# A two-block convolution on one core: a buffer of its own for each batch of d, its high part made by GpSimd, and a load of x without slots to wait for

## What is computed

```python
def _L0_conv_ref(x, p1, p3, p4, p5, p6):
    t1 = jnp.einsum('nchw,he->ncew', x, p1)             # h 32 -> e 16
    t2 = stack of x shifted by -1, 0, 1 rows            # 3c rows
    t3 = depthwise conv 9x9 of t1 with p3
    t4 = grouped conv 5x1 of t3 with p4, c // 4 groups
    t5 = jnp.einsum('ncew,ewf->ncf', t4, p5[:, :, 0, :])
    t6 = depthwise conv 1x3 of t5 along f with p6
    out = jnp.einsum('ncf,nfp->ncp', t6, t2) / sqrt(3c)

def _L1_conv_ref(x, conv_w, gamma, beta):
    cH, cV, cD = haar details of x; each upsampled bilinearly
    y = jnp.einsum('bchw,oc->bohw', concat([x, up(cH), up(cV), up(cD)]), conv_w)
    out = relu(batch norm of y * gamma + beta)

x = x + _L0_conv_ref(_gn(x), ...)
x = x + _L1_conv_ref(_gn(x), ...)
```

## Time and profile before

| | us |
|---|---|
| Median of 3 runs | 372.99 |
| Lowest, highest | 367.62, 376.11 |
| The profiled execution, its own time | 367.42 |
| Its span (first to last instruction) | 365.5 |
| TensorE, VectorE busy | 289.2, 294.2 |
| ScalarE, GpSimd busy | 215.3, 182.7 |

### The profile page before, as it was taken

One profiled execution on the slowest core, in us unless ns is written; L12 is line 12 of the kernel. 1 busy time (PEld: TensorE's weight loads), 2 busy tenths in 40 slices (PEclk: granted clock), 3 DMA queues, 4 the chain that ended last, 5 costly groups with the idle time before them and its releaser, 6 DMA issues.

```text
span 365.5 us, 4713 instructions
## 1 busy us (share of the span) xinstructions
PE 289.2 (79%) x1560; PEld 233.3 (64%) x1560; DVE 294.2 (81%) x539; ACT 215.3 (59%) x317; POOL 182.7 (50%) x186
## 2 busy tenths in 40 slices
PE   4566759999894994999989999999999999873000
PEld 0000129999783994567778888888888888651000
DVE  4899977985891862357668999999999999979792
ACT  3444665665963854364565667776676666530891
POOL 7454670050440040302487888888888888842000
PEclk9999998999999896999999999999999999995555
DMA  7979814589359761589000000000000000000399
GB/s 187 245 186 237 239 44 131 175 264 273 109 136 312 256 166 35 134 320 385 3 2 0 2 0 2 2 0 0 2 1 2 0 2 2 0 0 1 154 402 363
DMA packets 18344, 43.59 MB, mean 119 GB/s; under 512 B 2992, under 2 KB 7344, under 8 KB 18320
## 3 DMA queue, kind: packets, MB, share of 16 engines
q1 hardware_dynamic: 16928, 41.00, 36.6%
q0 software_dynamic: 960, 2.09, 2.3%
q10 hardware_dynamic: 432, 0.21, 0.2%
HBM read 30.44 MB, written 8.39 MB: 106 GB/s over the span
## 4 chain that ended last, share of the span: by engine, by line
DVE 48%; PE 21%; issue 8%; DMA 7%; SPq 6%; ACT 6%; POOL 3%; DVEq 0%; POOLq 0%; ACTq 0%
PE wide L637 10%; DVE xa L770 5%; DVE st L878 5%; DMA d_sb<-t_out 5%; DVE x_sb L983 4%; DVE x_sb L871 4%; DVE y_sb L917 4%; SPq L276 4%; DVE sty L923 3%; DVE sty L759 3%; DVE d_split L784 2%; DVE y_sb L910 2%; DVE u_sb L854 2%; DVE u_sb L846 2%; DVE u_sb L863 2%
## 5 line engine op out<-in xcount | busy, mean ns | idle before, releaser
L637 PE MATMUL wide<-t_all,s_hi 128*128 128x272 f32 x320 | 50.2, 306 | 15.5 <-ACT s_hi L465 12.9
L637 PEld LDWEIGHTS wide<-t_all,s_hi 128*128 128x128 f32 x320 | 45.2, 202 | 18.4 <-ACT s_hi L465 14.6
L778 DVE TENSOR_TENSOR s_lo<-s_f,s_hi 128x768 fp32r<-128x768 f32 x32 | 32.1, 1002 | 24.9 <-ACT s_hi L465 24.8
L429 POOL TENSOR_TENSOR g_lo<-y_sb,g_hi 128x1024 fp32r<-128x1024 f32 x15 | 36.2, 2411 | 14.4 <-ACT y_sb L562 14.4
L561 ACT ACTIVATE g_hi<-x_sb,rs 128x1024 fp32r<-128x1024 f32 x16 | 21.4, 1340 | 33.8 <-POOL rs L414 33.8
L607 PE MATMUL bank<-xa,p_blk 128*64 128x512 f32 x64 | 28.2, 979 | 14.8 <-DVE xa L770 14.8
L233 PE MATMUL wide<-g_hi,t_hi 128*128 128x512 f32 x96 | 38.0, 395 | 0.7 <-DVE t_lo L898 0.7
L276 POOL DMA_DIRECT2D d_sb<-t_out x24 | 13.3, 560 | 50.3 <-ACT t_out L479 43.9
L235 PE MATMUL wide<-g_hi,t_lo 128*128 128x512 f32 x96 | 37.7, 393 | 0.0
L234 PE MATMUL wide<-g_lo,t_hi 128*128 128x512 f32 x96 | 37.7, 392 | 0.0
L770 DVE STREAM_TRANSPOSE xa<-x_slot 128x1024 f32<-128x1024 f32 x16 | 31.6, 1993 | 6.6 <-DMA x_slot<-in_x 6.3
(11 more groups left out here) (130 smaller groups left out, 815.8 us busy)
## 6 DMA issues: line engine op xcount, KB each, us to landing
s_f<-in_taps SPq DMA_DIRECT2D x32, 384.0 KB, 4.8
x_sb<-in_x SPq DMA_DIRECT2D x8, 1024.0 KB, 7.8
x_slot<-in_x SPq DMA_DIRECT2D x28, 256.0 KB, 5.4
out<-x_sb SPq DMA_DIRECT2D x7, 1024.0 KB, 5.0
d_sb<-t_out POOLq DMA_DIRECT2D x24, 68.0 KB, 4.4
d_sb<-t_out SPq DMA_DIRECT2D x24, 68.0 KB, 5.1
x_slot<-in_x SPq DMA_DIRECT2D x8, 128.0 KB, 2.8
out<-x_sb SPq DMA_DIRECT2D x2, 512.0 KB, 2.7
```

Source lines behind the costliest of these rows:

```text
L429: pool.tensor_tensor(g2_lo[:, :], y_sb[:, n, :], g2_hi[:, :].bitcast(F32), ALU.subtract).then_inc(s["g2_lo"], 1)
L637: mm = pe.matmul(ps_t3[g % 2], weights[:, g % SR, 128 * t:128 * t + 128], t1_all[:, (2 * g + part) * JP + t:(2 * g + part) * JP + t + J, : ...
L778: dve.tensor_tensor(s_lo[:, g % SR, :], s_f[:, g % WR, :], s_hi[:, g % SR, :].bitcast(F32), ALU.subtract).then_inc(s["s_lo"], 1)
```

## The change

Three things are changed together.

1. **Load of x.** There are eight slots, one for each pair, and no wait between the loads. Three images' statistics are taken by ScalarE between its evacuations (`ACT_STATS_A`: after the 6th, 10th and 14th of 17), those of two more in groups 2, 4, 6 and 8 (`ACT_STATS_B`), each as two activations over the image with an accumulated sum (`x_moment`), the other eleven by VectorE after the transposes: eight halves before group 0, fourteen one by one in groups 0 to 13. The aggregation moves to groups 14 to 16, its product to 18, the scales to 27. p6, gamma and beta are loaded after the first taps.
2. **Buffers of d.** Each batch has its own `d_sb[b]`, in memory that t1 leaves; the shuffle waits for `d_groups[b]` groups (12, 15, 19 and 22, worked out from the sizes) instead of for `d_lo` of the batch before. `t4_out` and `d_sb` are laid out so that one transfer moves one run of 2176 bytes a partition. SP issues all 16 transfers of batches 0 to 2, four a step; of the last batch SP issues 6, GpSimd 5 and ScalarE 5. p5 now waits for 12 groups (8 before), since it lies behind `d_sb[0]`. x is loaded again later: pair 0 and `w_raw` after all shuffles of batch 2, pair 1 after those of batch 3, the rest when all of `d_lo` is made.
3. **The split of d.** GpSimd copies the high part, by `co` in place of `jc`: all of batches 0 to 2 and one piece of the last; ScalarE the other three. VectorE's remainders are spread over groups 18 to 30 (`D_LO_AT`) for batches 0 and 1, and come after the loop for batches 2 and 3. GpSimd's list is: batch 0, the power, batches 1 and 2, then its share of the last shuffle, two small memsets, its piece of batch 3.

The core of the diff:

```diff
-LATE = 6
-XR = 3
+BY_ACT = 5
+ACT_STATS_A = {5: 0, 9: 1, 13: 2}
+ACT_STATS_B = {2: (3, 0), 4: (3, 1), 6: (4, 0), 8: (4, 1)}
+EARLY = 8
+AGGR_AT, ST1_AT, GST_AT, RS1_AT = 14, 17, 20, 27
-SP_BLOCKS = 8
-RELOAD_AT = (27, 28)
-D_AT = (14, 22, 29)
+PER_STEP = 4
+LAST_SP, LAST_POOL = 6, 5
+BY_POOL = (4, 4, 4, 1)
+D_LO_AT = {18: (0, 0), 20: (0, 1), 22: (0, 2), 24: (0, 3), 26: (1, 0), 27: (1, 1), 29: (1, 2), 30: (1, 3)}
...
+        d_sb = [put("d_sb0", [CI, GB, JC, NO])]
         p5_raw = put("p5_raw", [JC, NF])
         end_raw = cursor[0]
+        ends_d = [end_raw]
+        for b in range(1, NB):
+            d_sb.append(put(f"d_sb{b}", [CI, GB, JC, NO]))
+            ends_d.append(cursor[0])
...
+        d_groups = [groups_below(end) for end in ends_d]
...
-        t4_out = put("t4_out", [2, JL, JC, GB, NO])
+        t4_out = put("t4_out", [2, JL, GB, JC, NO])
...
         def d_ready(eng, b):
             eng.wait_ge(s["t4_ev"], GB * (b + 1))
-            if b == 0:
-                eng.wait_ge(s["x_used"], 2 * N)
-            elif b < NB - 1:
-                eng.wait_ge(s["d_lo"], b)
+            eng.wait_ge(s["conv"], d_groups[b])
...
             for k in range(1, N // 2):
-                if k >= XR:
-                    sp.wait_ge(s["x_used"], 4 * (k - XR + 1))
-                load_x(sp, x_slot[k % XR][:, :, :], 2 * k, 2 * k + 2, x_in[k])
+                load_x(sp, x_slot[k][:, :, :], 2 * k, 2 * k + 2, x_in[k])
+                if k == N // 2 - 2:
+                    load_taps(sp, 0)
...
-            for step in range(G, G + SP_BLOCKS // 2):
+            for step in range(G, SHUFFLE_AT[-1] + len(blocks) // PER_STEP):
                 shuffle_step(step)
+            sp.wait_ge(s["d_lo"], CI)
+            sp.wait_ge(s["conv"], x_groups)
+            reload_x(sp, 0)
+            stats_done(sp)
+            sp.dma_start(w_raw[:, :, :], w_in).then_inc(s["w_raw"], 16)
             d_ready(sp, NB - 1)
-            shuffle(sp, NB - 1, blocks[:7], d_in[NB - 1])
+            shuffle(sp, NB - 1, blocks[:LAST_SP], d_in[NB - 1])
             sp.wait_ge(s["conv"], G)
...
+            d_split_pieces(0, range(BY_POOL[0]))
+            pool.wait_ge(s["gst"], 1)
+            pool.tensor_tensor(rs1[:, 1, :], rs1[:, 0, :], minus_half[:, :].broadcast_to([128, N]),
+                               ALU.pow).then_inc(s["gst_q"], 1)
+            d_split_pieces(1, range(BY_POOL[1]))
+            d_split_pieces(2, range(BY_POOL[2]))
+            d_ready(pool, NB - 1)
+            shuffle(pool, NB - 1, blocks[LAST_SP:LAST_SP + LAST_POOL], d_in_pool)
...
+            def x_moment(n, k, junk):
+
+                func, scale = ((ACT.Identity, 1.0 / HW), (ACT.Square, 1.0 / W))[k]
...
+                act.activation(junk, x_slot[n // 2][:, n % 2, :], func, scale=scale,
+                               accum_out=mv1[:, n, k:k + 1]).then_inc(s["act_stats"], 1)
...
                 if g == GB:
-                    act.wait_ge(s["x_used"], 2 * N)
+                    act.wait_ge(s["act_stats"], 2 * 2)
                 if b >= 2 and g % GB == 0:
                     wait_d(act, b - 2)
...
-                for b in range(NB - 1):
-                    if D_AT[b] <= g < D_AT[b] + JC:
-                        d_high(b, g - D_AT[b])
...
+            def d_low(b, co):
+                if co < CI - BY_POOL[3] and b == NB - 1:
+                    dve.wait_ge(s["d_hi"], co + 1)
+                else:
+                    dve.wait_ge(s["d_pool"], CI * b + co + 1 if b < NB - 1 else sum(BY_POOL))
+                src, hi, lo = split_views(b, co)
+                dve.tensor_tensor(lo, src, hi.bitcast(F32), ALU.subtract).then_inc(s["d_lo"], 1)
```

More of the change, by code:

```diff
@@ L121, in build @@
         p5_groups = groups_below(end_raw)
-        x_groups = [groups_below(at_x + 4 * HW * 2 * (k + 1)) for k in range(N // 2)]
+        d_groups = [groups_below(end) for end in ends_d]
+        x_groups = groups_below(at_x + 4 * HW * 2)
         cursor[0] = end_t
@@ L131, in build @@
         cursor[0] = end_t
-        x_slot = [put("x_slot2", [2, HW])]
+        x_slot = [put(f"x_slot{k}", [2, HW]) for k in range(1, N // 2 - 1)]
         xa = put("xa", [2, W, G])
@@ L195, in build @@
         ps_o, ps_y = wide
-        names = ("const ones pads zeros w_raw p5_raw p6_in p1_in xa x_used t1_mm t1_hi t1_f t1_lo "
-                 "w_det w_f w_hi w_lo s_hi s_lo conv t3_hi t3_lo t4_mm t4_ev d_hi d_lo p5_hi p5_lo u_part "
+        names = ("const ones pads zeros w_raw p5_raw p6_in p1_in xa x_used act_stats t1_mm t1_hi t1_f t1_lo "
+                 "w_det w_f w_hi w_lo s_hi s_lo conv t3_hi t3_lo t4_mm t4_ev d_hi d_lo d_pool p5_hi p5_lo u_part "
                  "st1 gst_mm gst gst_q rs1 t5 u_act u t6_mm t6_hi t6_lo g1_f g1_hi g1_lo o_half o_mm x1 "
@@ L205, in build @@
         d_in = [sem(f"s_d_in{b}") for b in range(NB)]
-        d_in_pool = [sem(f"s_d_in_pool{b}") for b in range(NB)]
+        d_in_pool = sem("s_d_in_pool")
         s_in = [sem(f"s_s_in{r}") for r in range(WR)]
@@ L470, in _ @@
                 t1_high(i)
+                if i in ACT_STATS_A:
+                    for k in range(2):
+                        x_moment(ACT_STATS_A[i], k, wide[0][:, :])
             def t4_evacuate(g):
@@ L501, in _ @@
                     act.copy(p5_hi[:, jc, :], p5_raw[:, jc, :]).then_inc(s["p5_hi"], 1)
-                for b in range(NB - 1):
-                    if D_AT[b] <= g < D_AT[b] + JC:
-                        d_high(b, g - D_AT[b])
             t4_evacuate(G - 1)
             d_ready(act, NB - 1)
-            shuffle(act, NB - 1, blocks[13:], d_in[NB - 1])
-            for jc in range(G - D_AT[NB - 2], JC):
-                d_high(NB - 2, jc)
-            for jc in range(JC):
-                d_high(NB - 1, jc)
+            shuffle(act, NB - 1, blocks[LAST_SP + LAST_POOL:], d_in[NB - 1])
+            for co in range(CI - BY_POOL[3]):
+                d_high(3, co)
             def middle_of_u(k):
```

163 lines of the change are left out of this document (80 added, 83 removed).

## The result

| | before | changed |
|---|---|---|
| Median, us | 372.31 (4 runs) | 361.12 (4 runs) |
| Lowest, highest | 367.62, 376.11 | 359.17, 363.56 |
| Profiled execution, its span | 367.42, 365.5 | 360.26, 358.4 |

The profiled execution of the kernel before is its fastest, 4.9 us under its median; that of the changed kernel is 0.9 us under its own. So 4 us of the 11 lie outside what the traces can explain. 356 was forecast, in a range of 346 to 367.

What follows compares the result with a forecast made beforehand. TensorE waits for ScalarE, stuck in `d_high` for d's shuffle, losing 19.4 us. Load -2.6, group stage -12.4, d path's end +1.7: -13.3 from 367.4 gives 354.1; with a third of the median's offset 356, range 346 to 367.

Steps and rivals of the forecast that it cites:

- the median's offset: Whole kernel: earlier runs' median lay 5.6 us above the profiled execution; a third was taken, making 354.1 into 356.
- the rival of the unmoved wait: Groups 16 and 24: `t4_evacuate` still waits on ScalarE for a whole batch, 1 to 4 us each, 359; chance 0.12.
- the bound of 5.2: Load stage: the most it could shorten, -5.2 us, if ScalarE hid all of its added statistics.
- Single activations: Groups 2, 4, 6, 8: ScalarE's added activations delay it 0.4 us each, 1.7 us together (0 to 4 x 1.35).
- SP's term: Group stage near group 14: taps late behind p5's longer wait, then steps of four shuffles and a load; 3 us (0 to 6).
- The rival that the issue of a shuffle gets cheaper with one run of 2176 B: SP's shuffles: issue falls from 0.603 to 0.33 us, saving 3 us; with another 3 elsewhere, 350; chance 0.15.
- the one of a bound queue: SP's queue becomes the bound: 0.45 us more on each of 32 shuffles in the group stage, 365; chance 0.13.
- Batches 1 and 2, and the copies beside VectorE: Group stage: SP's issuing excess for batches 1 and 2, 0.8 us (0 to 4); GpSimd's copies holding VectorE up, 1.5 (0 to 6).
- Its full price of some 8 us: Group stage: VectorE and GpSimd lock each other out at every copy, 14.4 us less VectorE's slack, in place of 1.5.
- chain (b): End of d path: GpSimd's last shuffles queue behind four batch 2 copies; first t5 about 15.3 us after last product, +1.7.
- Chain (a): End of d path: warming waits for pair 0 of x behind batch 2's shuffles, 1.7 to 3.8 us late; 14.8 to 16.9.
- named as a thing that would prove me wrong: Whole kernel: the prediction is wrong if the granted clock stays below 1 where TensorE doesn't stand still.

Runs made afterwards that it cites:

- The shared-buffer run: The changed kernel with the shuffles of batches 1 and 2 waiting for the batch before's remainders, batch 0 and 1 remainders moved earlier: 382.55 us, ratio 1.0309.
- the last two versions: Changed kernel with combined edits (ScalarE high parts, early p5, GpSimd sharing shuffles, late pair 1), pair 0 after group 29's taps, then after group 31's: 355.83 and 354.46 us.

## Why the prediction was right, and where it was off

**The forecast was 354.1 + 1.9 for the median's offset; measured are 360.26 + 0.9.** The sum over the stages missed by 6.2 us, half of the gain forecast between the traces: -1.2 in the load stage, +3.2 in the group stage, +2.45 at the end of the d path, +1.8 in the last stage. That 361 still lies well inside the range is owed to its width, not to the sum.

**The mechanism and the sign were right.** All of `d_high`'s waits left the group stage, and `t4_evacuate` did not wait in their place (the rival of the unmoved wait falls: ScalarE waits for d once, at the end). The shared-buffer run shows that it needs the own buffers.

**Load stage: -3.8, said -2.6, for another reason.** ScalarE was to end it. What ends it is the transfer. VectorE and TensorE in the changed kernel:

```profile
40.62 3.84 DVE L797 STREAM_TRANSPOSE xa<-x_slot 128x1024 f32<-128x1024 f32 x2 [2.12 <-DMA x_slot<-in_x]
...
42.63 1.62 PE L633 MATMUL bank<-xa,p_blk 128*64 128x512 f32 x4 [3.00 <-DVE xa L797]
```

The last pair landed at 40.6, where 39.8 was said, and the transposes end at 44.46 ("near 44"). The term that was mis-sized is ScalarE's, above all its evacuations: they were counted at 1.07 + 0.63 us each, but the second instruction starts before the first ends, and where they follow one another they start 1.41 us apart (at 23.89, 25.28 and 26.71), 3.2 us less over eleven, of which 0.4 had been allowed for. The moments, by form:

```profile
L492 ACT ACTIVATE wide<-x_slot 128x1024 f32<-128x1024 f32 x6 | 6.2, 1034 | 0.1
...
L492 ACT ACTIVATION_READ_ACCUMULATOR wide<-x_slot 128x1 f32 x6 | 1.2, 195 | 0.0
```

That is 1.23 us for both instructions, as said (1.25), without the waits that were added. So ScalarE had time over: it waited for TensorE four times after 28 us, 2.7 us in all, and its last evacuation ends at 48.05, not 49.2. The transposes end 4.4 us earlier than before (the bound of 5.2, less 0.8 for the later landing), and 0.6 of it is lost behind them. By these rows nearly all of that is TensorE's clock: after 3.0 us of standing still it was granted 0.5 from 43.0 us on, and the last product but one took 1.62 us where 1.08 was the time before (ScalarE waits for it and runs without a pause from 44.29 on).

The 3.8 is also one draw. In the eleven profiles with this load code the second part of group 0 starts at 48.8 to 52.2 us, with the landing of the last pair, 50.2 on average: 3.4 us under the one profile of the kernel before.

**Single activations: 1.0, said 1.7** (four times 0.4 is 1.6). Groups 4, 6, 8 and 10, two behind each pair of activations, lose 0.25 each (0.24 to 0.28 in every run here).

**SP's term, the largest miss in the group stage: 5.9, said 3.** The hole at group 14 was sized rightly: taps out 23.8 us after conv(2) (said 23.1), 2.8 us lost (1.4 to 3.8 by the landings). What failed is the step "2.74 us, 0.46 more than a group" for what follows: groups 15 to 17 lose 3.1 and not 1.4. A step of four shuffles and a load was counted at 2.74 us; it takes 3.1 to 3.3, since the load takes 0.58 us to issue behind shuffles and not 0.33, and four shuffles 2.41 to 3.05. The run with the early p5 takes 3.0 us of the 5.9 away, all of it at group 14; GpSimd's help with the issuing takes another 1.4 to 2.1. What the DMA share of 1.02 to 1.06 adds at 84 to 98 us is not shown apart from these: at 1.00 with the issuing shared TensorE had no gap. The rival that the issue of a shuffle gets cheaper with one run of 2176 B falls: four take 2.41 us, 0.60 each, as in the earlier trace rows. So does the one of a bound queue: there is no general 0.45 us more on each.

**Batches 1 and 2, and the copies beside VectorE: 2.95, said 0.8 + 1.5.** Near in size, but the cause isn't shown: with no copy on GpSimd and ScalarE's casts in the same groups, as much was lost (3.45). A copy on GpSimd took more than said. By form, in the changed kernel:

```profile
L802 DVE TENSOR_TENSOR s_lo<-s_f,s_hi 128x768 fp32r<-128x768 f32 x32 | 31.9, 996 | 13.8 <-ACT s_hi L481 13.7
...
L392 POOL CAST d_split<-d_sb 128x544 fp32r<-128x544 f32 x13 | 20.5, 1684 | 63.0 <-DMA d_sb<-t_out 63.0
```

1.68 us on average against 1.2, from 1.1 to 3.1; three of the thirteen took over 2 us, which was named as a sign of being wrong, though their mean is below it. The one that runs with VectorE idle takes 1.32. `s_lo` stays at 0.996 on average (1.002 in the earlier trace rows), for it meets a copy only now and then. The rule of the Trainium skill that the prediction weighed ("SBUF — State Buffer", "Who interferes with whom") is seen in this case: VectorE takes 0.61 and 0.96 us for eleven elements beside a copy. Its full price of some 8 us is not seen, because only instructions that meet pay it.

**Group stage in sum.** Said 19.4 won less 7.0; measured 19.4 less 1.0, 5.9 and 2.95, or 9.5 (9.2 by the windows, the difference lies in the pace, 2.26 or 2.28).

**The end of the d path: +4.15, said +1.7.** Three terms of chain (b) failed: the last landing, the price of the copies, and the remainders. POOL, ScalarE and VectorE in the changed kernel:

```profile
132.70 6.00 POOL L392 CAST d_split<-d_sb 128x544 fp32r<-128x544 f32 x4 [10.80 <-DMA d_sb<-t_out]
138.57 2.71 POOL L285 DMA_DIRECT2D d_sb<-t_out  x5
```

```profile
136.22 16.02 PE L696 MATMUL bank<-x_sb,g_mean 128*128 128x384 f32 x40 [2.21 <-DMA x_sb<-in_x]
...
145.47 3.23 ACT L516 CAST d_split<-d_sb 128x544 fp32r<-128x544 f32 x3 [11.02 <-DMA d_sb<-t_out]
145.52 1.32 POOL L392 CAST d_split<-d_sb 128x544 fp32r<-128x544 f32 x1 [3.98 <-DMA d_sb<-t_out]
146.83 4.53 DVE L811 TENSOR_TENSOR d_split<-d_sb,d_split 128x544 fp32r<-128x544 f32 x4 [6.15 <-ACT d_split L516]
```

Chain (b), which sets it, in the terms of the prediction (us):

| | said | measured |
|---|---|---|
| batch 2 lands, after the last product | 0.3 | -1.3 |
| four copies | 4.8 | 5.9 |
| five issues | 3.0 | 2.7 |
| to land | 3 | 4.2 |
| casts and remainders | 4.3 | 5.9 |
| to the first t5 | 0 | 0.4 |
| sum | 15.4 | 17.8 |

Batch 2 landed 1.6 us after the end of its last issue, where 4.3 was taken. The landing of the last batch met pair 1's load, issued by SP at 138.27, just ahead of GpSimd's shuffles; the prediction named pair 1 nowhere in its sum. Of the copies it had the price too low. The casts and remainders: four remainders in a row behind the first cast (1.36 + 4.53), not three casts and one remainder. Chain (a) was right on its start, 2.2 us late (1.7 to 3.8 was said; 10.3 + 5.3 is 15.6 and not 16.0, so the lower end should read 1.3), and wrong on its length: TensorE stood still 2.2 us, the granted clock fell to 0.5, and the 20 products took 16.02 us where they took 13.06. So the two chains end together, the warming products at about 152.2 and the remainders at 151.4, and the early pair 0 gained nothing by itself. In the kernel with the early p5 the remainders end at 148.6 and the first t5 starts at 149.46: there the slow warming products are the later chain.

**The last stage: +1.8, said 0.** Between 306 and 309 us, in the last step over the images, the granted clock is at its lower level while TensorE works (the two windows at the end of the first fence), and nine products take 0.63 us instead of 0.40; that is 1.55 us of it, the rest is lost in the first products of t5. This was named as a thing that would prove me wrong. The dip is in 8 of the 14 profiles of this study. In the others first t5 to the end is 204.7 to 204.8 us instead of 206.3 to 206.7, with two special cases: the run with pair 0 alone early has no dip and still takes 206.6, since its first products of t5 ran at the lower clock after 4.85 us of standing still, and the run with doubled copies has both (207.9). The gaps just before the dip are the same (0.93 and 0.66 us in the changed kernel, 0.98 and 0.63 in the kernel before, which has no such dip), and no edit switches it plainly: it is absent in the kernel before, in the runs with VectorE's statistics, with pair 0 early and with pair 1 late, and in the last two versions, and present in the rest. Its cause stays open.
